# The direct term D*u: fp32 products with diagonals, or a scaled copy and accumulating transposes

## What is computed

```
u = silu(conv(x_in))                    # 512 channels
s[t] = exp(delta[t] * A) * s[t-1] + delta[t] * B[t] * u[t]      # 16 states a channel
y[t] = sum over n of s[t, n] * C[t, n]
y = y + u * D                           # the direct term, D one number a channel
y = y * silu(z);  out = y @ W_out
```

## Time and profile before

| | |
|---|---|
| median of the runs | 2422.21 us |
| the profiled execution, its span | 2425.2 us |
| VectorE busy | 2038.4 us, 84% |
| TensorE busy (its weight loads) | 2186.3 us, 90% (1766.3, 73%) |
| GpSimd busy | 1827.8 us, 75% |
| ScalarE busy | 1506.5 us, 62% |
| scan part, end | some 1810 us |

### The profile page before, as it was taken

One profiled execution on the slowest core, in us unless ns is written; L12 is line 12 of the kernel. 1 busy time (PEld: TensorE's weight loads), 2 busy tenths in 40 slices (PEclk: granted clock), 3 DMA queues, 4 the chain that ended last, 5 costly groups with the idle time before them and its releaser, 6 DMA issues. The chain is left out here.

```text
span 2425.2 us, 47399 instructions
## 1 busy us (share of the span) xinstructions
PE 2186.3 (90%) x13721; PEld 1766.3 (73%) x13722; DVE 2038.4 (84%) x3037; ACT 1506.5 (62%) x3292; POOL 1827.8 (75%) x1093
## 2 busy tenths in 40 slices
PE   8889899998989898998989898999787999999980
PEld 5667677677777666777777776767676999999970
DVE  5999999999999999999999999999974555555558
ACT  6687877878786877878787878877741111111106
POOL 3888989889898989889888989898962434444447
PEclk9999999999999999999999999999987999999995
DMA  5041322314041323324041413223137998999978
GB/s 172 7 134 54 131 75 102 124 52 164 21 158 48 131 69 114 106 70 153 32 156 34 144 49 135 80 96 116 62 123 199 226 228 229 229 230 229 229 166 277
DMA packets 186791, 312.50 MB, mean 129 GB/s; under 512 B 18851, under 2 KB 118083, under 8 KB 186500
## 3 DMA queue, kind: packets, MB, share of 16 engines
q1 hardware_dynamic: 140932, 258.53, 33.4%
q0 software_dynamic: 25584, 34.62, 7.5%
q10 hardware_dynamic: 20112, 17.32, 2.2%
HBM read 247.09 MB, written 63.32 MB: 128 GB/s over the span
## 5 line engine op out<-in xcount | busy, mean ns | idle before, releaser
L855 POOL TENSOR_TENSOR dbu<-drive_u,b_rows 128x1024 f32<-128x1024 f32 x384 | 904.3, 2363 | 87.7 <-DVE ps_a L660 35.1
L1159 ACT ACTIVATE ps_a<-delta,a_neg 128x512 f32<-128x512 f32 x768 | 517.2, 685 | 136.9 <-DVE ss L660 120.2
L872 POOL TENSOR_TENSOR wp<-ss,rows_c 128x1024 f32<-128x1024 f32 x192 | 453.6, 2363 | 37.6 <-DVE ss L660 36.9
L1766 POOL DMA_INDIRECT acc_scratch<-ow,idx x135 | 211.2, 1564 | 309.2 <-issue 102.4
L672 DVE TENSOR_TENSOR wd<-ps_a,rows_c 128x1024 f32<-128x1024 f32 x320 | 383.3, 1198 | 0.0
L1437 PEld LDWEIGHTS ps_y<-ident,wd 128*128 128x128 f32 x2560 | 299.4, 143 | 98.7 <-issue 70.5
L1437 PE MATMUL ps_y<-ident,wd 128*128 128x128 f32 x2560 | 337.3, 277 | 12.4 <-DVE wd L672 12.4
L1804 ACT COPY e_meta<-xt 128x2 f32<-128x2 f32 x135 | 25.9, 192 | 439.0 <-PE e_ps_x L1877 294.4
L1464 PEld LDWEIGHTS ps_a<-dg,duT 128*128 128x128 f32 x2048 | 248.6, 196 | 60.6 <-issue 58.1
L1464 PE MATMUL ps_a<-dg,duT 128*128 128x128 f32 x2048 | 259.0, 281 | 31.6 <-ACT carry L1166 28.6
L1688 DVE TENSOR_SCALAR e_hT<-e_ps_h,b_turned 128x128 f32<-128x128 f32 x540 | 152.1, 344 | 144.7 <-PE e_ps_h L1886 125.2
(11 more groups left out here) (200 smaller groups left out, 3653.8 us busy)
## 6 DMA issues: line engine op xcount, KB each, us to landing
b_rows<-in_L_ffn_W_dram SPq DMA_DIRECT2D x135, 512.0 KB
rows_c<-b_scratch SPq DMA_DIRECT2D x128, 512.0 KB, 4.9
b_rows<-b_scratch SPq DMA_DIRECT2D x96, 512.0 KB, 4.1
xt<-xs_scratch SPq DMA_DIRECT2D x135, 129.0 KB
xb<-in_L_attn_x_dram SPq DMA_DIRECT2D x16, 512.0 KB, 4.0
hx<-in_L_attn_x_dram SPq DMA_DIRECT2D x16, 512.0 KB, 6.3
x_scratch<-hx SPq DMA_DIRECT2D x16, 512.0 KB, 2.9
acc_scratch<-stage SPq DMA_DIRECT2D x16, 512.0 KB, 2.9
```

What stands on the lines that cost most here:

```text
L855: pool.tensor_tensor(dbu[:, k % NBU], du[:, g % 2, :].unsqueeze(1).broadcast_to([P, 2, CH]), bb[:, row:row + 2, :], ALU.mult).then_inc(dbu ...
L872: pool.tensor_tensor(wp[:, s % 2], ss[:, s % 2], cc[:, rows, :], ALU.mult).then_inc(wp_done, 1)
L1159: act.activation(dst, dl[:, g, :], ACT.Exp, scale=a_neg[:, g, n:n + 1]).then_inc(exp_done, 1)
L1766: pool.indirect_dma_start(out=acc_dram, out_offset=bass.IndirectOffsetOnAxis(ap=idx[:, old, :], axis=0), in_=ow[:, old, :], in_offset=None ...
```

## The change

The diagonals of D go. ScalarE makes D*u, channel-major, into one new buffer `ud` of 128x512 (the size of `skipd`), by one scaled copy a group at n=3 (`SKIP_U`), just before the exponential of that step. `begin_y` waits for it in the place of reading u itself, and transposes it into `ps_y` with four accumulating transposes. Two semaphores guard `ud`.

```
-        skipd = sb("skipd", [P, G, P])
+        ud = sb("ud", [P, CH])
+        SKIP_U = 3
# VectorE, at the start
                 for k in range(TAPS):
-                    dve.tensor_scalar(taps[:, g, k, :], ident[:], cw[:, g, k:k + 1], None, ALU.mult)
-                ins = dve.tensor_scalar(skipd[:, g, :], ident[:], dp[:, g:g + 1], None, ALU.mult)
+                    ins = dve.tensor_scalar(taps[:, g, k, :], ident[:], cw[:, g, k:k + 1], None, ALU.mult)
# ScalarE
+            def skip_term(t):
+                if t > 0:
+                    act.wait_ge(ud_turned, t)
+                act.wait_ge(u_done, t // G + 1)
+                act.activation(ud[:], xslot(t // G, t % G), ACT.Copy, scale=dp[:, t % G:t % G + 1]
+                               ).then_inc(ud_done, 1)
...
                     for k in keep_at.get(at, ()):
                         keep(k)
+                    if s % N == SKIP_U:
+                        skip_term(c * G + s // N)
                     exp_a(c, s // N, s % N)
# TensorE, begin_y
                     pe.wait_ge(gated, t)
-                u = xslot(t // G, t % G)
+                pe.wait_ge(ud_done, t + 1)
                 for i in range(NT):
-                    pe.matmul(ps_y[:, i, :], u[:, i * P:(i + 1) * P], skipd[:, t % G, :], start=(i == 0), stop=False,
-                              skip_group_check=True)
+                    ins = pe.matmul(ps_y[:, i, :], ud[:, i * P:(i + 1) * P], ident[:], start=(i == 0), stop=False,
+                                    is_transpose=True, skip_group_check=True)
+                ins.then_inc(ud_turned, 1)
```

More of the change, by code:

```diff
@@ L261, in mamba_block @@
         gated = sem("gated")
+        ud_done = sem("skip_term_made")
+        ud_turned = sem("skip_term_turned")
         x1_out = sem("x1_stored")
```

## The result

The changed kernel takes 2442.18 us, the median of four runs (2441.56 to 2443.21), where the kernel before takes 2422.39 us beside it (four runs, 2421.08 to 2423.82). The ratio is 1.0081, with a 95% interval from 1.0069 to 1.0093: 19.8 us slower. The forecast was 2431.0 us, 8.8 us slower, in a range from 2417 to 2443: the direction is right, the measured time is 0.8 us inside the upper end of the range, and the difference is 2.2 times the forecast one.

What follows compares the result with a forecast made beforehand. VectorE was taken to set the scan part's pace, ScalarE or TensorE binding some stretches. Even chunks +5.2, odd +1.1, chunks 0 and 15 +0.9 make +7.2; clock +1.6 gives +8.8 on 2422.2: 2431.0 us, range 2417 to 2443.

Steps and rivals of the forecast that it cites:

- VectorE sets the pace: In the scan part a chunk is VectorE's work plus its waits, with some stretches bound by ScalarE or TensorE.
- The copy, 0.60 us of ScalarE: Each new scaled copy, one a group, holds ScalarE's queue 0.60 us; bounds 0.52 and 0.75 us.
- Its cost at s=3: Copy at step 3 of a chunk's 64, in the stretch ScalarE bounds: +0.54 us in even chunks.
- The wait at s=10 grows from 1.75 to 2.3 us: At step 10 of a chunk VectorE waits for ScalarE's logarithm; the copy at s=3 was to lengthen this wait.
- rival 2: ScalarE's gaps absorb the copy, so -0.45 us stays in each of 15 chunks: -6.8 us, 2415.4 us; chance 0.08.
- Odd chunks at s=3: The copy at step 3 of odd chunks costs +0.47 us, a 0.13 us gap before ScalarE's evacuation being filled.
- The transposes, -0.45 us at s=23: The second group's transposes, in the stretch TensorE bounds, save 0.45 us a chunk; the other three groups' save nothing.
- s=40 and s=54: Late steps of a chunk: +0.35 us at s=40 and +0.3 at s=54 in even chunks, +0.15 at s=40 in odd.
- Rival 3: Nothing measurable: s=10 and s=23 cancel, small waits eat the later pushes; +0.1 us a chunk, 2424 us; chance 0.18.
- The start, chunk 0 and chunk 15: Ends of the scan part: start 0, chunk 0 +0.4 us, chunk 15 +0.5 us.
- The clock: TensorE's clock falls to half level at s=39 to 42 in four even chunks; one more fall expected, +1.6 us.
- Rival 1: Products at s=39 and s=55 held the clock up; without them ten more falls, 16 us, 2445 us; chance 0.15.

Runs made afterwards that it cites:

- e3: The changed kernel with each copy moved into the group before, at s=15, 31, 47 and 63; 2426.51 us, ratio 1.0017 to before.
- e1: The changed kernel with its four transposes turned back into fp32 products with the identity, the copy kept; 2442.54 us, ratio 1.0075 to before.
- e2: The kernel before with its products replaced by transposes of u itself, no copy (output lacks factor D); 2407.61 us, ratio 0.9936 to before.
- e12: e2 with three idle VectorE instructions added a chunk, 0.84 us; 2433.48 us, ratio 1.0039 to before.
- e7: e2 with the copy added at s=3, 19 and 51, none for the third group; 2430.98 us, ratio 1.0025 to before.
- e4: The change for the second group of a chunk alone, copy at s=15, the other groups keeping their products; 2412.06 us, ratio 0.9950 to before.
- e13: e2 with six idle VectorE instructions once, at s=60 of chunk 3, about 1.7 us; 2417.38 us, ratio 0.9975 to before.

## Why the prediction was right or wrong

The time lies in the range and on the side that was forecast. The parts:

- **VectorE sets the pace, and which stretch is bound by what: right.** Every edit moved the time where the stretches said: s=3 to 10 ScalarE, s=25 TensorE, s=40 ScalarE's evacuation.
- **The copy, 0.60 us of ScalarE: right**, 0.61 in the trace.
- **Its cost at s=3: right in size, wrong in place.** "The wait at s=10 grows from 1.75 to 2.3 us" is the step that failed. The copy stands ahead of the exponential of n=3, and VectorE's scan of that state was so close behind that it now waits there, 0.43 us; with VectorE and ScalarE both later by the same amount, the wait at s=10 stays at 1.75. By the prediction's own test ("The forecast is wrong if s=10 doesn't grow (rival 2)") a reader would have called it wrong. The test was too narrow, since what had to be watched is the sum of the waits from s=3 to s=10. e3 shows the cost: with the copy moved, +0.54 becomes 0.00.
- **Odd chunks at s=3: sized too low**, +0.61 against +0.47 (1.0 us in seven chunks). The gap of 0.13 us in front of the evacuation at 602.06 did not absorb anything.
- **The transposes, -0.45 us at s=23 and nothing elsewhere: right**, by the wait at s=25 (2.14 to 1.69, and 1.64 to 1.19 in odd chunks), and by e1, where it is missing, and e2, where it stands alone. The three other groups gained nothing but 0.03 us a chunk at s=40 (e2). The factor is two, 0.88 to 0.44 us.
- **s=40 and s=54: right** (+0.31 and +0.42 in even chunks, +0.10 in odd ones).
- **Rival 2**, which had the copy absorbed, is out: +0.54 came through. Rival 3 as well: s=3 and s=23 nearly cancel (+0.12 to +0.15 us a chunk), but the pushes at s=40 and s=54 were not eaten.
- **The start, chunk 0 and chunk 15: +0.9 forecast, -0.9 measured**, and together with +7.9 for +6.3 in chunks 1 to 14 this makes +7.0 for +7.2. The agreement of the two sums is partly luck.
- **The clock: the term of the sum that was mis-sized.** "With them gone I expect the same or a few more falls; one is in the sum" was +1.6 us. The profiled executions have five more, 7.8 us, and the medians are further apart by 3.5 us than the spans, which no trace explains. The reason given was wrong too: removing the products of s=39 takes no clock away there (e2). What fits all runs is that the change made the chunks longer and so changed when each comes, as idle work alone does in e12; that this is how the changed kernel's five came about is inferred from e12 and e7, not shown by itself, and the cause stays open that far. Rival 1 came near the measured time (2445 against 2442.2) by a mechanism that e2 refutes.

## What to carry to other kernels

Where a stretch is bound by one engine, work moved from a slack engine into that stretch is paid in full, whatever the engine's average: the copy was 0.6 us on an engine with 22 us free a chunk and cost 0.54 of it; with the same copy in a gap (s=15) it costs nothing there, though e3 as a whole, with its eight falls, is 0.17% over before. Limited to the group whose term lies in TensorE's stretch the change wins 0.5% (e4), somewhat over half of it by its work and the rest by fewer falls. Before a few us are put down to an edit, count the clock's falls in both traces and take them out of the difference; here they were half of it, and they came with idle work alone too; only falls at a step for which another engine waits count. When a test for a predicted wait is written, it should name the stretch over which the wait may appear, not one instruction.

## What was not expected of the hardware

- Equal rows of TensorE, within 0.01 us for 55 us (before, chunks 2 and 4), once with the clock kept behind them and once with it at the half level.
- One delay of 1.7 us in 2400 goes with a median 9.8 us higher and a spread of 13.5 us where it was 2 (e13 against e2); that the delay is the cause is not shown.
- 0.84 us of idle VectorE work a chunk cost 1.6 us a chunk (e12 against e2), in a kernel whose other engines have the same work.
